# First scores alternated between two banks and moved behind the turned maxima; 512-column rounded products in the waits

## What is computed

```
# layer 2, for every expert e: h = u * sigmoid(u) * v;  out += (h @ W3[e]) * weights[..., e]
Q = (decoder_input @ W_q).reshape(B, Sd, HEADS, HEAD_DIM)     # B 4, Sd = Se = 256, 16 heads of 8
K = (encoder_output @ W_k).reshape(B, Se, HEADS, HEAD_DIM)
V = (encoder_output @ W_v).reshape(B, Se, HEADS, HEAD_DIM)
scores = jnp.einsum('bqhd,bkhd->bhqk', Q, K) / jnp.sqrt(jnp.float32(HEAD_DIM))
attn = jax.nn.softmax(scores, axis=-1)
out = jnp.einsum('bhqk,bkhd->bqhd', attn, V).reshape(B, Sd, E)
return out @ W_o + b_o
```

## Time and profile before

| | us |
|---|---|
| three runs | 211.35, 208.94, 211.54; median 211.35 |
| the profiled execution | 208.93, of which its span 207.2 |
| TensorE busy | 179.9 (87% of the span) |
| VectorE busy | 141.6 (68%) |
| ScalarE busy | 102.9 (50%) |
| GpSimd busy | 36.8 (18%) |

### The profile page before, as it was taken

How to read it: one execution, slowest core, us unless ns; L and a number is a source line. 1 busy time by engine, 2 the same in 40 slices (tenths; PEclk the granted TensorE clock), 3 DMA queues, 4 the chain that set the end, 5 groups by cost and what they waited for, 6 DMA issues and landing times.

```text
span 207.2 us, 3930 instructions
## 1 busy us (share of the span) xinstructions
PE 179.9 (87%) x1410; PEld 141.7 (68%) x1410; DVE 141.6 (68%) x404; ACT 102.9 (50%) x184; POOL 36.8 (18%) x52
## 2 busy tenths in 40 slices
PE   5699899899999999999999999788878887889331
PEld 4389598678799988888888887545556654557210
DVE  2899758667467556746455958669778867875684
ACT  2266478444423222532336225966785587547243
POOL 3734274624000000400000003500000000004400
PEclk9979999999999999999999999999999999999955
DMA  6993000000000000000000000000000000000002
GB/s 200 391 413 126 5 2 0 0 3 0 0 0 5 0 0 3 0 0 0 3 0 0 0 5 0 0 3 0 5 0 0 3 3 2 0 3 2 0 0 101
DMA packets 3330, 6.61 MB, mean 32 GB/s; under 512 B 880, under 2 KB 2160, under 8 KB 3056
## 3 DMA queue, kind: packets, MB, share of 16 engines
q1 hardware_dynamic: 1440, 5.51, 6.8%
q10 hardware_dynamic: 1872, 0.87, 1.5%
HBM read 5.84 MB, written 0.52 MB: 31 GB/s over the span
## 4 chain that ended last, share of the span: by engine, by line
PE 71%; DVE 15%; issue 5%; ACT 3%; POOL 3%; DMA 1%; DVEq 0%; POOLq 0%; ACTq 0%
PE banks L1126 12%; PE bank L1197 7%; PE bank L1162 6%; PE bank L948 6%; PE bank L950 5%; PE bank L949 5%; DVE negm L798 4%; PE banks L1184 3%; PE bank L1170 3%; PE banks L949 2%; PE banks L948 2%; PE banks L950 2%; PE bank L1206 2%; PE bank L1126 2%; POOL rstd L246 2%
## 5 line engine op out<-in xcount | busy, mean ns | idle before, releaser
L798 DVE TENSOR_REDUCE negm<-bank 128x2 f32<-128x512 f32 x60 | 39.6, 688 | 14.2 <-PE bank L1162 13.9
L456 ACT ACTIVATE raw<-banks 128x1024 f32<-128x1024 f32 x32 | 31.0, 1020 | 22.3 <-PE banks L1184 22.3
L419 ACT ACTIVATE att<-bank 128x512 f32<-128x512 f32 x32 | 19.1, 598 | 45.3 <-PE bank L950 32.6
L1162 PE MATMUL bank<-stk 32*128 32x256 f32 x120 | 22.3, 313 | 0.2 <-DVE negm L798 0.2
L777 DVE SCALAR_TENSOR_TENSOR xs<-banks,rw,xs 128x128 f32<-128x128 f32 x56 | 15.8, 344 | 7.8 <-PE banks L1126 7.7
L1162 PEld LDWEIGHTS bank<-stk 32*128 32x128 f32 x120 | 14.5, 183 | 9.2 <-issue 7.9
L948 PE MATMUL bank<-xT,w 128*128 128x512 f32 x48 | 20.1, 420 | 0.5 <-DVE xT L706 0.5
L1126 PEld LDWEIGHTS banks<-raw,attT 128*128 128x128 f32 x160 | 19.2, 192 | 1.2 <-issue 0.5
L1126 PE MATMUL banks<-raw,attT 128*128 128x128 f32 x160 | 19.7, 276 | 0.0
L950 PE MATMUL bank<-xT,w 128*128 128x512 f32 x48 | 18.8, 392 | 0.0
L244 POOL TENSOR_SCALAR vpe<-mv 128x4 f32<-128x4 f32 (+1 forms) x9 | 2.4, 268 | 92.4 <-DVE mv L575 92.2
(11 more groups left out here) (202 smaller groups left out, 371.0 us busy)
## 6 DMA issues: line engine op xcount, KB each, us to landing
raw<-in_w SPq DMA_DIRECT2D x1, 2048.0 KB, 10.4
raw<-in_w SPq DMA_DIRECT2D x1, 1024.0 KB, 9.2
xs<-in_x SPq DMA_DIRECT2D x2, 256.0 KB, 3.2
ctxT<-in_ctxT SPq DMA_DIRECT2D x1, 512.0 KB, 5.3
ctx<-in_ctx SPq DMA_DIRECT2D x1, 512.0 KB, 6.4
wl<-in_wl SPq DMA_DIRECT2D x1, 256.0 KB, 7.2
picks<-in_sel ACTq DMA_DIRECT2D x1, 256.0 KB, 11.5
out<-cT SPq DMA_DIRECT2D x1, 256.0 KB, 2.1
```

Of the source, the lines that this page charges most:

```text
L419: act.activation(silus[:, k, :], bk[2 * k][:, :], ACT.Silu).then_inc(S["silu_s"], 1)
L456: act.activation(probs[:, m % 2, 2 * r:2 * r + 2, :, :].rearrange("p h k q -> p (h k q)"), pair[r][:, :], ACT.Exp, scale=ATT_SCALE).then_i ...
L798: dve.tensor_reduce(negm[:, m % 2, :, c0:c0 + 1].rearrange("p t c -> p (t c)"), bk[score_bank(m, r)][:, :].rearrange("p (t k) -> p t k", t ...
L1162: ins = pe.matmul(bk[score_bank(m, r)][:, t * SEQ:(t + 1) * SEQ], stk[rows, m % G, t * P:(t + 1) * P], stk[rows, m % G, SEQ:2 * SEQ], star ...
```

## The change

- `score_bank` gives the first scores of a group to banks 1 and 2 in turn: r = 0 and r = 2 in one, r = 1 and r = 3 in the other, where the turned maxima of the group ahead lie. For group 0, r = 0 to 2 stay in bank 6 and r = 3 goes to bank 1.
- On TensorE `scores(m + 1, 0)` now stands directly behind `turn_maxima(m)`; `scores(m + 1, 1)` and the picks behind the shifted scores; `scores(m + 1, 3)` ahead of `outputs(m - 1)`.
- On VectorE `shifted(m)` stands ahead of `maxima(m + 1, 0)`, where it stood behind it; `maxima(m + 1, 1)` stands ahead of `normalise` and `add_attention`.
- `scores(0, 3)` moves ahead of `down(13)`, and `maxima(0, 3)` right behind `maxima(0, 2)`. `turn_maxima(0)` and `scores(1, 0)` move ahead of `down(14)`. `weigh(13)`, `weigh(14)` and `weigh(15)` move down: 13 and 14 into group 0, 15 into group 1.
- `fill` issues products of 512 columns with rounded float32 operands (fp32r) into bank 3, again unread; `FILLED` gives one in groups 1, 7, 8, 11, 12 and 14 and two in group 2, all ahead of the shifted scores; two more stand in group 3 and four at the end of group 1. They take the place of the `keep_warm` calls in groups 0, 1, 2, 7 and 11. The `keep_warm` calls of group 15 and behind it stay.
- On ScalarE `exps(2, 0)` and `exps(2, 1)` move ahead of the four `third_scaled`.

```diff
--- before.py
+++ after.py
@@ -31,7 +31,7 @@
 GROUPS = G * BATCH
 QUAD = 32
 SHIFT_ROW = 24
-WARMED = {1: 3, 2: 3, 2 * G - 1: 2, 3 * G - 1: 2}
+FILLED = {1: 1, 2: 2, 2 * G - 1: 1, 2 * G: 1, 3 * G - 1: 1, 3 * G: 1, 3 * G + 2: 1}
 TURNED_AT = (2 * G - 1, 3 * G - 1, 3 * G + 2)
 WARM_UP = 4
 EPS = 1e-5
@@ -180,8 +180,8 @@
 
         def score_bank(m, r):
             if m == 0:
-                return 6
-            return 2 - m % 2 if r == 2 else 1 + m % 2
+                return 6 if r < HPG - 1 else 1
+            return 1 + (m + r) % 2
 
         def turn_bank(b, t):
             return 0 if b == BATCH - 2 or (t == 0 and b == BATCH - 1) else 7
@@ -475,11 +475,11 @@
                     queries_hi(1)
                 if m in TURNED_AT:
                     turned_out(b - 1)
+                exps(m, 0)
+                exps(m, 1)
                 if m == 2:
                     for t in range(*HALVES[1]):
                         third_scaled(t)
-                exps(m, 0)
-                exps(m, 1)
                 if m >= 1:
                     o_copy(m - 1)
                 if m + 3 < GROUPS:
@@ -828,9 +828,13 @@
             def dve_group(m):
                 b, g = m // G, m % G
                 more = m + 1 < GROUPS
+                shifted(m)
                 if more:
                     maxima(m + 1, 0)
-                shifted(m)
+                if m < 2:
+                    weigh(UNITS - 3 + 2 * m)
+                if more:
+                    maxima(m + 1, 1)
                 if m == G:
                     queries_lo(1)
                 if g == 0 and b >= 2:
@@ -840,13 +844,9 @@
                 if 0 < b < BATCH - 1 and g == 2:
                     normalise(b - 1, 1)
                 if more:
-                    maxima(m + 1, 1)
+                    maxima(m + 1, 2)
                 if m == 0:
                     weigh(UNITS - 2)
-                if more:
-                    maxima(m + 1, 2)
-                if m == 0:
-                    weigh(UNITS - 1)
                 if m == 1:
                     sum_moments(HALVES[1])
                 if more:
@@ -873,7 +873,7 @@
                     dve.wait_ge(S["setup"], 1)
                 if n >= UNITS - 2:
                     maxima(0, 2 * (n - UNITS + 2))
-                if n >= 2:
+                if 2 <= n < UNITS - 1:
                     weigh(n - 2)
                 if n >= UNITS - 2:
                     maxima(0, 2 * (n - UNITS + 2) + 1)
@@ -961,6 +961,10 @@
                 for _ in range(count):
                     pe.matmul(bk[bank][:, 0:P], ident, ident, start=True, stop=True)
 
+            def fill(bank, count):
+                for _ in range(count):
+                    pe.matmul(bk[bank][:, :], w12[:, 0, 0, 0:P], xT[:, 0, 0:HALF], start=True, stop=True)
+
             pe.wait_ge(S["setup"], 1)
             for _ in range(WARM_UP):
                 pe.matmul(bk[7][:, 0:SEQ], negm[:, 0, 0, :], negm[:, 1, :, :].rearrange("p t c -> p (t c)"),
@@ -1149,14 +1153,17 @@
 
             def scores(m, r):
                 pe.wait_ge(S["stack_s"], m + 1)
-                if m == 0:
+                if m == 0 and r == HPG - 1:
+                    pe.wait_ge(S["hid_s"], HB * (UNITS - 1) + 1)
+                elif m == 0:
                     pe.wait_ge(S["s1_max"], r)
                 elif r == 0:
-                    pe.wait_ge(S["s1_max"], 4 * m - 1)
-                elif r == 2:
+                    pe.wait_ge(S["hid_s"], HB * UNITS)
+                    pe.wait_ge(S["s1_max"], 4 * m)
+                elif r == 1:
                     pe.wait_ge(S["qa_s"], m)
                 else:
-                    pe.wait_ge(S["s1_max"], 4 * m + (r + 1) // 2)
+                    pe.wait_ge(S["s1_max"], 4 * m + r - 1)
                 rows = slice(QUAD * r, QUAD * (r + 1))
                 for t in range(TPB):
                     ins = pe.matmul(bk[score_bank(m, r)][:, t * SEQ:(t + 1) * SEQ], stk[rows, m % G, t * P:(t + 1) * P],
@@ -1226,10 +1233,9 @@
                 if m >= 2:
                     pe.wait_ge(S["o_ev"], m - 1)
                 if m == 3:
+                    pe.wait_ge(S["p_s"], 2 * m - 1)
+                    fill(3, 2)
                     turn("ln3", "x3T_ps", 7, 1)
-                if m in WARMED:
-                    pe.wait_ge(S["p_s"], 2 * m - 1)
-                    keep_warm(3, WARMED[m])
                 if m == G:
                     project_queries(1)
                 if g == 0 and 2 <= b:
@@ -1264,32 +1270,34 @@
             def pe_group(m):
                 more, final = m + 1 < GROUPS, m == GROUPS - 1
                 turn_maxima(m)
+                if more:
+                    scores(m + 1, 0)
+                if m == 0:
+                    down(UNITS - 2)
                 if not final:
                     bank7_used(m)
+                if m in FILLED:
+                    pe.wait_ge(S["p_s"], 2 * m - 1)
+                    fill(3, FILLED[m])
+                shifted_scores(m)
                 if more:
                     scores(m + 1, 1)
                 if 0 < m < GROUPS - 3:
                     pick_group(m + 3)
-                shifted_scores(m)
                 if more:
                     scores(m + 1, 2)
                 if m == 0:
                     down(UNITS - 1)
+                if more:
+                    scores(m + 1, 3)
+                if m == 0:
                     pick_group(3)
-                    pe.wait_ge(S["p_s"], 1)
-                    keep_warm(3, 4)
                 if m >= 1:
                     bank7_free(m)
                     outputs(m - 1)
-                if more:
-                    scores(m + 1, 3)
-                if m == 0:
-                    keep_warm(3, 4)
-                if m + 2 < GROUPS:
-                    scores(m + 2, 0)
                 if m == 1:
-                    pe.wait_ge(S["p_s"], 3)
-                    keep_warm(3, 5)
+                    pe.wait_ge(S["p_s"], 2 * m + 1)
+                    fill(3, 4)
                 if m == 3 * G + 1:
                     pe.wait_ge(S["ao_s"], TPB * (BATCH - 2) + 1)
                     turn_outputs(BATCH - 2, 1)
@@ -1326,14 +1334,13 @@
                     pick_group(n - UNITS + 3, 7)
                 if n >= UNITS - 2:
                     scores(0, 2 * (n - UNITS + 2))
+                if n == UNITS - 1:
+                    scores(0, HPG - 1)
                 down(n - 2)
                 if n == 3:
                     logits(1)
-                if n >= UNITS - 2:
-                    scores(0, 2 * (n - UNITS + 2) + 1)
-            pe.wait_ge(S["hid_s"], HB * UNITS)
-            scores(1, 0)
-            down(UNITS - 2)
+                if n == UNITS - 2:
+                    scores(0, 1)
             for m in range(GROUPS):
                 pe_group(m)
             outputs(GROUPS - 1, 1)
```

## The result

| | before | changed |
|---|---|---|
| median of the executions, us | 210.99 | 235.78 |
| all four | 211.35, 208.94, 211.54, 210.62 | 234.79, 235.87, 248.09, 235.69 |
| profiled execution and its span | 208.93, 207.2 | 234.79, 233.0 |
| mean granted clock of TensorE | 0.969 | 0.836 |

The changed kernel takes 1.118 times as long (95% interval 1.111 to 1.124). The forecast was 210.4 in a range of 206.9 to 214.0, with 0.14 for the case that came: the clock fell.

The account below looks back on a forecast made before the run. The prediction took a circle through PE and DVE, neither full, to bound the kernel. At full clock, 208.93 less 1.35 gained early plus 2.9 lost in groups 5 to 14 gave 210.4 us, range 206.9 to 214.0.

Parts of the forecast that it names:

- The sum of 210.4: Whole execution at full clock: 208.93 less 1.35 gained up to group 4, plus 2.9 lost in groups 5 to 14.
- the circle: Attention groups: the limit runs through PE and DVE in turn, neither full; before the change some 4.2 us a group.
- Groups with g = 1 and 2: Within groups 5 to 14, those with `normalise` between DVE's maxima: 1.28 + 2.72 + 0.50 = 4.50 us each.
- A: Time from a group's turn of the maxima to the start of its shifted scores: 1.28 us with g = 1 and 2.
- g = 0 or 3: Other groups from 5 on: 4.66 us for g = 0 (`add_attention`, a fill), 4.24 for g = 3 (no DVE extra).
- The lone pair: Next group's first pair of scores, alone on PE behind the turned maxima: 0.43 us by the row, 0.22 by the page.
- The first rival: Pair of first scores costs only 0.22 us where it now stands: 207.2 us in all, 0.8% faster; chance 0.25.
- The start: Group 0 and the last `down` steps: turn of group 1 at 120.8, not 123.49, so 2.7 us gained.
- Groups 1 to 4: Stretch behind the start: part of its gain is given back, turn of group 5 at 141.1 against 142.46, 1.35 left.
- Group 3's stall: PE waits from 131.5 to 132.1 us, as `bank7_used(3)` needs `o_copy(1)`, queued on ScalarE behind exponentials and `third_scaled`.
- The clock rival: TensorE's clock falls in the attention: about 1.5 us a group, one group 212, from three on 215 or more; chance 0.14.
- the second rival: Groups 5 to 14: DVE waits only for the turn, most groups 3.9 us, 203.5 in all; chance 0.06.

Follow-up runs that it names:

- the old products back at the start: Changed kernel with the old identity products back in groups 0 to 2 in place of the new ones: 239.71, 233.45, 234.51 and 215.79 us.
- the kernel with more products: Changed kernel with more unread 512-column products in groups 0 to 14, ahead of the shifted scores: 222.23 to 229.63 us, median 224.11.
- the one with the old product: Changed kernel with each 512-column product replaced by a 128-column identity product, same places and counts: 235.71 us once, 247.48 to 250.52 in three.
- the old order with longer groups: Kernel before plus an unused 1024-column VectorE sum ahead of the fourth maxima of groups 4 to 14: 216.65, 226.61, 232.24 and 233.06 us.
- Products in the waits: Kernel before with the change's start and identity products in TensorE's waits, groups 2 to 12: median 207.58 us; without those on the path in 2, 7, 11: 207.35.
- the new product in the old places: Kernel before with the identity products of groups 0, 1, 2, 7 and 11 replaced by 512-column ones: 214.56 to 215.66 us in three executions, 210.14 in one.

## Why the prediction was wrong

The step that failed is the one by which the forecast set the low clock aside: "PE stays busy about three quarters of each group, near what groups 3 and 4 had at clock 1.00". The sum of 210.4 had the low clock at nothing; it took some 18 to 24 us, an estimate from the executions of one kernel with and without the long fall (the old products back at the start). The other terms together were about 2 us too small.

- **What bounds the kernel, and the circle.** Right. Groups with g = 1 and 2 were to take 4.50 and took 4.59 and 4.58; A was to be 1.28 and is 1.38; DVE's idle ahead of the second maxima was to be 0.46 and is 0.56. The changed loop is slower at full clock, as the sum had it. From group 5 on the changed kernel has no group with g = 0 or 3 that stood at full clock throughout, so their 4.66 and 4.24 were not tested in it.
- **The lone pair.** 0.43, as the row said, and not the 0.22 that the Trainium skill ("TensorE: Matmul & The Clock Gate", "Back-to-back issue gap") gives by its 262 cycles for 256 columns, an estimate. The first rival falls.
- **The start.** Turn of group 1 forecast 120.8, measured 120.65. Counted from `up(15)` (108.08 before, 108.25 here) it came 3.0 earlier, where 2.7 was forecast.
- **Groups 1 to 4.** Turn of group 5 forecast 141.1, measured 143.85. Group 3's stall is there and its 5.42 is near the 5.3 of the sum; group 1 took 7.82 in place of 5.7, as the clock was low from 122.5. In the kernel with more products, where the clock held, it took 5.77 with more work. So here too the sum was right and the clock failed it.
- **The clock rival.** Named, with its place and the side on which it ends, but given 0.14, priced too low and counted too short. The price was 1.5 us a group and is 2.5 (7.06 against 4.59). The forecast slowed only the 2.0 us of PE's work that lie in the circle; at low clock the whole group is PE's (busy 7.04 of 7.06 in groups 10 and 11), and the values' product, 1.96 in place of 1.09, counts in full. And the range had one group at the low clock, the rival three or more. The clock was low for 54.6 us in the changed kernel and for over 100 in the one with the old product.
- **The sentence against it.** In groups 5 and 6 of the changed kernel PE is busy 7.92 of 9.17 us, 0.86, not three quarters, and more than the 6.77 of 8.26 before, 0.82; and the clock falls in group 7, right behind them. At low clock PE is busy 0.96 and the clock does not rise. The busy share of the profile neither warned of the fall nor told when it would end. A clean trace was no evidence of distance from the edge either: seven of the 41 executions of the same kernel lost some of their clock.
- **The range** was built from a clock that holds, or is lost for one group. (Its high end adds up to 212.8 + 1.5 = 214.3, and the second rival to 208.93 - 3.0 - 2.7 = 203.2; neither changes the outcome.) The execution of 215.8 that kept its clock tells how much the rest of the sum missed. It is 5.4 above the median of the kernel before beside it. The sum had 1.5, and the products put back in group 0 are 1.8 more (8.49 against 6.66). So about 2 us, an estimate, were under-counted in the loop at full clock, 0.1 of it in each group with g = 1 or 2.
- **The rule on cycling through banks** (the Trainium skill, the same page, "A second HAM failure mode: psum-queue depth-cycling") tells of a clock that swings where there are short idles between groups of products. The rows agree as far as a fall goes. In the changed kernel the clock stays low rather than swings; in the old order with longer groups it fell and came back twice.

What stays open: which property of the work the clock follows. Longer groups with the same work made the long fall frequent (three of four executions above 226, against two of 41), so neither the kind of product nor the new order is needed for it. Products in the waits made it rare (none of 15 executions above 211, against two of four above 214 without them). The measure behind this is not shown. It was not tried to fill the new loop's own wait ahead of the fourth pair (0.65, until 146.85): ScalarE reads the banks of the shifted scores from 145.78 to 147.72.

## What to carry to other kernels

A change that makes a loop longer by a tenth at the same work of TensorE is to be priced with its clock first: look how long the loop would take at half clock, and take into account that it may stay there. Here that was worth 18 to 24 us, against some 3.5 for everything else (the 1.5 of the sum and the 2 that it missed). Try unread products in the waits that the trace shows rather than on the path: here they cost nothing and the clock held, by the times and mean clocks, in all but one of 15 executions. And take many executions before trusting a clean clock in one. The four executions of the kernel before that stand beside the result, 208.94 to 211.54, gave no warning; the spread of all 41, 208.9 to 241.0, does.

## What the runs showed of the hardware that was not expected

- The low clock can hold while TensorE is busy nearly all the time: 34.98 of 36.36 us (changed) and 97.50 of 102.70 (old product), at 0.50 throughout. In other traces it ended by itself after 3.4 us (the old order with longer groups) up to 17 us (the new product in the old places).
- The same program fell or did not from one execution to the next: 215.79 and 239.71, 208.40 and 238.07, 209.09 and 241.03.
- Half a clock does not double a group: 7.06 against 4.59. A group is then nearly all PE (busy 7.04 of 7.06 in groups 10 and 11), and DVE's extras are hidden again: group 10, with `normalise`, and group 11, without, both take 7.06.
- A busy stretch does not keep the clock: the first fall of the changed kernel, at 122.5, came behind a stretch in which PE was busy 5.21 of 5.30 us (117.0 to 122.3).
